# A graph network's tensor convolution: GpSimd folds a group's products in two halves between indirect transfers

## The reference

```python
R = relu(abs_distances[:, None] @ w1 + b1) @ w2 + b2        # 384 radial weights an edge
Fj = features[src]                                          # gathered source rows
for i, (mo, lo) in enumerate(RS):                           # RS = [(8, 0), (8, 1)]
    acc = zeros((E, mo, 2 * lo + 1))
    for j, (mi, li) in enumerate(RS):
        for k, lf in enumerate(range(abs(lo - li), lo + li + 1)):
            acc += _NORM[i] * einsum('euv,ef,evi,ofi->euo', Rb[..., k], Yf, Fb, C)
    msg_blocks.append(acc.reshape(E, -1))
out = zeros(...).at[dst].add(concatenate(msg_blocks, axis=-1))
```

## Time and profile before

| what | value |
|---|---|
| median of 3 runs | 21268.92 us (21262.17 to 21287.74) |
| the profiled execution's own time | 21112.0 us |
| its span, first to last instruction | 21110.3 us |
| granted TensorE clock, mean | 0.846 |
| DVE busy over the whole span | 13900.8 us (66%) |
| POOL busy over the whole span | 10869.3 us (51%) |
| folds L2815 | 808, 1021.0 us in all |

### The profile page before, as it was taken

One profiled execution on the slowest core, in us unless ns is written; L12 is line 12 of the kernel. 1 busy time (PEld: TensorE's weight loads), 2 busy tenths in 40 slices (PEclk: granted clock), 3 DMA queues, 4 the chain that ended last, 5 costly groups with the idle time before them and its releaser, 6 DMA issues. The chain is left out here.

```text
span 21110.3 us, 373963 instructions
## 1 busy us (share of the span) xinstructions
PE 12868.1 (61%) x82322; PEld 11031.7 (52%) x82323; DVE 13900.8 (66%) x32034; ACT 8909.7 (42%) x19928; POOL 10869.3 (51%) x11458
## 2 busy tenths in 40 slices
PE   1333332323433333333799488888887888888887
PEld 1233232323333333333788455555556888888887
DVE  5167674112222222222788599989998999999999
ACT  5521121111000000000799288868884555555554
POOL 2677776664666666666211100000005888888887
PEclk9999999999555555555899699999998999999998
DMA  2111111112222222222455233323332222222223
GB/s 61 14 16 15 15 15 15 14 14 16 59 58 58 58 58 59 58 58 58 46 49 49 45 105 105 105 88 105 105 105 49 45 45 45 45 45 45 45 45 42
DMA packets 2940091, 1096.13 MB, mean 52 GB/s; under 512 B 2414118, under 2 KB 2633479, under 8 KB 2938505
## 3 DMA queue, kind: packets, MB, share of 16 engines
q1 hardware_dynamic: 2510328, 650.25, 16.0%
q0 software_dynamic: 312576, 231.97, 6.8%
q10 hardware_dynamic: 117044, 212.38, 3.3%
HBM read 999.36 MB, written 98.48 MB: 52 GB/s over the span
## 5 line engine op out<-in xcount | busy, mean ns | idle before, releaser
L2795 POOL DMA_INDIRECT conv_far<-conv_rows x3232 | 3074.0, 951 | 2876.1 <-DMA att_far_all<-rows_by_src 2023.9
L819 POOL DMA_INDIRECT weighted_far<-in_x_dram,weighted_rows x3232 | 3305.1, 1023 | 1840.4 <-issue 987.2
L1557 POOL DMA_INDIRECT rows_by_src<-push_row,push_index x3232 | 3165.0, 979 | 1668.8 <-issue 1564.6
L909 PE MATMUL weighted_total<-weighted_message,weighted_hot 128*128 128x33 f32 x6464 | 1498.5, 399 | 3359.8 <-issue 2009.9
L1633 PE MATMUL push_near<-far_rows_sb,push_turned 128*128 x6464 | 1677.7, 434 | 2853.5 <-issue 2132.6
L909 PEld LDWEIGHTS weighted_total<-weighted_message,weighted_hot 128*128 128x128 f32 x6464 | 1433.0, 328 | 3426.1 <-issue 3425.1
L1633 PEld LDWEIGHTS push_near<-far_rows_sb,push_turned 128*128 128x128 f32 x6464 | 1577.4, 328 | 2900.6 <-issue 2899.9
L1407 PE MATMUL hop_sums_ps<-hop_hots,place_i 128*96 128x512 bf16 x11904 | 2827.9, 380 | 388.1 <-issue 382.5
L2916 PE MATMUL conv_radial_a<-radial,conv_hidden 128*128 128x256 f32 x6464 | 2676.1, 500 | 369.1 <-DVE conv_products_b L3054 243.9
L1333 DVE TENSOR_SCALAR hop_hots<-hop_wide_iota,hop_nodes 128x512 bf16<-128x512 f16 x10416 | 2849.6, 339 | 2.3 <-PE hop_sums_ps L1407 2.3
L1592 DVE TENSOR_TENSOR push_place<-push_place,push_trash 128x4 f32<-128x4 f32 x808 | 131.8, 163 | 3450.9 <-DMA push_place<-place_by_dst 3117.6
(11 more groups left out here) (353 smaller groups left out, 24941.4 us busy)
## 6 DMA issues: line engine op xcount, KB each, us to landing
hop_line<-sources_of_tiles SPq DMA_DIRECT2D x744, 512.0 KB
push_line<-local_by_group ACTq DMA_DIRECT2D x808, 256.0 KB
conv_weights<-weight_by_group SPq DMA_DIRECT2D x808, 128.0 KB
att_far_all<-rows_by_src SPq DMA_DIRECT2D x880, 80.0 KB
weighted_rows<-edges_by_dst SPq DMA_DIRECT2D x3232, 4.0 KB
weighted_far<-in_x_dram,weighted_rows POOLq DMA_INDIRECT x3232
push_place<-place_by_dst SPq DMA_DIRECT2D x3232, 0.5 KB
rows_by_src<-push_row,push_index POOLq DMA_INDIRECT x3232
```

The costliest lines, as they stand in the source:

```text
L819: pool.indirect_dma_start(far[s][:, j, :], None, table, bass.IndirectOffsetOnAxis(ap=rows[s][:, j, 0:1].bitcast(I32), axis=0)).then_inc(ga ...
L909: last = pe.matmul(total[:].rearrange("p n c -> p (n c)")[:, bass.ds(at[s % SLOTS * HALVES + j // COLUMNS], width)], hot[b][:, j, :], mess ...
L1557: pool.indirect_dma_start(k.rows_by_src, bass.IndirectOffsetOnAxis(ap=index[s][:, j:j + 1], axis=0), row[s][:, j, :], None).then_inc(writt ...
L2795: pool.indirect_dma_start(far[s][:, j, :], None, k.conv_dram, bass.IndirectOffsetOnAxis(ap=rows[s][:, j, 0:1].bitcast(I32), axis=0)).then_ ...
```

## The change

GpSimd's fold is cut in two along the columns. Before, one addition of 128 by 512 stood after the second of a group's four transfers. Now an addition of 128 by 256 (columns 0 and 1) stands after the first transfer, and another (columns 2 and 3) after the third. Only the first waits for `products_made`. Each adds 1 to `folded`, and `finish_a` waits for twice the count, that is, for both halves. After the loop the last two groups' halves follow one another with no transfer between.

```diff
-                gather(s, range(PER // 2))
-                if fold:
-                    fold_products()
-                gather(s, range(PER // 2, PER))
-
-            def fold_products():
-
-                pool.wait_ge(products_made, 1)
-                pool.sem_clear(products_made)
-                pool.tensor_tensor(folded_a[:], products_a[:, :, :, 0:MUL], products_a[:, :, :, MUL:2 * MUL],
+                for half in range(2):
+                    gather(s, range(half * (PER // 2), half * (PER // 2) + 1))
+                    if fold:
+                        fold_products(half)
+                    gather(s, range(half * (PER // 2) + 1, (half + 1) * (PER // 2)))
+
+            def fold_products(half):
+
+                if half == 0:
+                    pool.wait_ge(products_made, 1)
+                    pool.sem_clear(products_made)
+                cut = slice(half * (PER // 2), (half + 1) * (PER // 2))
+                pool.tensor_tensor(folded_a[:, cut], products_a[:, cut, :, 0:MUL], products_a[:, cut, :, MUL:2 * MUL],
                                    ALU.add).then_inc(folded, 1)
...
             for s in range(AHEAD):
-                fold_products()
+                for half in range(2):
+                    fold_products(half)
...
-                dve.wait_ge(folded, i * SLOTS + s + 1)
+                dve.wait_ge(folded, (i * SLOTS + s + 1) * 2)
```

## The result

The changed kernel takes 21525.25 us in the median (21507.17 to 21536.28, 4 runs) against 21278.33 us (21262.17 to 21295.77, 4 runs): 1.0112 times as long, 95% interval 1.0100 to 1.0124. It is 247 us slower. The forecast was 155 us slower, 21424 us.

What follows compares the result with a forecast made beforehand. VectorE's own work was taken to bound the convolution at 6.21 us a group. A 0.194 us wait at `finish_a` in 798 groups adds 155 us to the 21269 us median, giving 21424 us; range 21310 to 21530 us.

Steps and rivals of the forecast that it cites:

- What bounds the kernel: Convolution: VectorE's own work, 6.20 to 6.21 us a group, sets the period; GpSimd has about 0.07 us to spare.
- the slack of 2.39 us: Kernel before: time from the whole fold's end on GpSimd to the start of `finish_a` on VectorE.
- A half fold: GpSimd's addition over half the columns: 0.717 us predicted, with a fixed part of 0.17 us.
- From half to half: GpSimd, first half's end to second half's start: two transfers and their gaps, 2.38 us.
- the signal: GpSimd's release of VectorE after the second half: 0.04 us, so `finish_a` starts at 3.85 us, due at 3.66.
- The ring: Fold to `finish_a` to next fold, without a buffer: 3.85 + 2.55 = 6.40 us a group, against 6.21.
- The sum: Whole convolution: 798 of 808 groups each pay 0.194 us, +155 us, giving 21424 us.
- the first rival: At `finish_a`: second half ready after all, wait 0.053 us or less, not slower; at f = 0 (no fixed part) +22 us; chance 0.07.
- The second half in time: At `finish_a`: the second half's result comes early enough, wait 0.053 us or less, not slower; chance 0.07.
- a gain: Convolution faster through a cheaper exchange of GpSimd's gaps: at most 0.01 us a group, 8 us in all; chance 0.02.
- The late transfer: Group's last transfer, now behind the second half, lands late: 0.2 us more a group, some 21585 us; chance 0.05.
- The wait is larger: At `finish_a`: GpSimd's release of VectorE costs 0.23 us, wait 0.38 us, +306 us, 21575 us; chance 0.13.

## Why the prediction was right, and where it was short

**What bounds the kernel, and the slack of 2.39 us.** Right. The runs with one, two and three transfers between the halves turn on it.

**A half fold, 0.717 us.** Measured 0.728 us, 0.011 more in each half.

**From half to half, 2.38 us, and the signal, 0.04.** Measured 2.39 us (18004.62 to 18007.01) and 0.03. The `finish_a` start of 3.85 us was 3.87.

**The ring.** Right: a period of 6.42 us for the 6.40 said, 7.67 for 7.68 with one more transfer. The steady part is 168 us for the 155 of the sum; GpSimd idles 0.2 us ahead of the first half, as said.

**The sum.** Here a term was missing, and that the time still lies in the range is partly luck. I let each group cost the same, and took it that moving GpSimd's wait ahead of a group's second transfer cost nothing since the count of transfers from one release to the next stays four. The change also put that wait where something in GpSimd's instruction stream stalls every 26 groups. That is worth 69 us. The median of 21525 us lies 101 us above my 21424: 69 are the pauses, 13 the larger ordinary wait, 9 the fourth run of the kernel before, which raised its median, and 10 stay unassigned. It lies near the top of the range, inside it only by room given for a larger signal, which was not larger. Two small slips changed nothing: the four transfers of the earlier trace rows add up to 3.80 us and not 3.82, and the wait of the first rival at f = 0 is 0.02 us and not 0.03. No rival named this. In the traces of the kernel before there was no row that showed it.

**Rivals.** The second half in time and a gain are out, since `finish_a` waits in nearly each group. The late transfer is out, since L3000 has no idle time. "The wait is larger" is not what happened either: the ordinary wait was 0.21 us, and the excess sits in 30 groups.

**Why the pause is hidden in the kernel before** is argued, not shown: its trace has no row of the stall. GpSimd's sequencer runs ahead of its transfers: of the two groups below (start times of its semaphore clears, the kernel before, one period), the fold's clear comes at 18008.7 and the next group's first clear at 18010.0, while the transfers that stand between them in the code run until 18012.48.

```profile
L2814 POOLq EVENT_SEMAPHORE_RANGE_CLEAR  x1: 44/44/44, 18008.7 to 18008.7; - x1
L2803 POOLq EVENT_SEMAPHORE_RANGE_CLEAR  x1: 44/44/44, 18010.0 to 18010.0; - x1
```

It can then hand over the next group's first two transfers long before they run, and stands waiting for the products until 18014.9. A stall of 2.4 us of the sequencer at the second transfer fits into that. In the changed kernel the wait stands ahead of that transfer, nothing is handed over in advance, and the stall is bare. The run with five transfers supports this: its trace shows the same 2.4 us of delay with no gap between transfers. The same clears in the changed kernel, in an ordinary group and in one with a pause:

```profile
L2816 POOLq EVENT_SEMAPHORE_RANGE_CLEAR  x1: 44/44/44, 18048.7 to 18048.7; - x1
L2803 POOLq EVENT_SEMAPHORE_RANGE_CLEAR  x1: 44/44/44, 18050.4 to 18050.4; - x1
...
L2816 POOLq EVENT_SEMAPHORE_RANGE_CLEAR  x1: 44/44/44, 18055.1 to 18055.1; - x1
L2803 POOLq EVENT_SEMAPHORE_RANGE_CLEAR  x1: 44/44/44, 18059.2 to 18059.2; - x1
```

1.7 us from one to the other in the first, 4.1 in the second: the sequencer is 2.4 us late, not only the transfer. What the runs show is that the pause needs the wait between the first and the second transfer (the change, the late `finish_a`, one and three transfers between, the whole fold earlier and the wait moved alone have it; the kernel before, the adjacent halves, and the halves one later have none), and that the transfer then starts 3.17 us after the released fold. The wait there isn't enough: the run with five transfers has it and no pause. What makes the sequencer stall stays open: it comes every 26 groups or 104 transfers with four transfers a group, every 20 groups or 100 transfers with five, so neither count is the cause by itself.

## What to carry to other kernels

When a consumer waits for a piece of work, what counts is the latency from the producer's signal to that piece's end. Cutting the piece in two and letting other work in between adds all of that work to the latency, and if the consumer closes a ring with no buffer in it, what exceeds the slack is paid in every round: here 3.66 us stood against 3.87. The slack must be read between the end of the piece on one engine and the start of its consumer on the other, since neither engine's busy share shows it. And a wait that is moved along an in-order queue changes what can be handed over ahead of it: look not only at how much stands between two waits, but at which instructions now stand right behind one.

## What the runs showed of the hardware

- GpSimd's addition of 128 by 512 took 1.263 us and of 128 by 256 took 0.728: a fixed part of 0.19 us. The Trainium skill, GPSIMD Engine Reference, section Elementwise, gives about 2.6 cycles an element. An estimate from that figure, at the page's 1.2 GHz, puts the fixed part at 0.15 us; the measurement decides for 0.19.
- A VectorE instruction that waits on GpSimd starts 0.03 us after the end of GpSimd's record.
- On VectorE, an instruction that reads what the one directly ahead wrote started 0.23 us later than one that doesn't (0.59 against 0.36 us behind a 128 by 288 product).
- With the wait for the products behind a group's first indirect transfer, the second one started 3.31 us after GpSimd's clear behind that wait instead of 1.01, once in 26 groups of four transfers. With five transfers a group the clears were 2.4 us late once in 20 groups, and no transfer was. The cause is open.
